# Sparse cross-attention and a trigonometric FFN on one core: thresholds in three Newton rounds, a reordered end, and two moved synchronisations

## The reference

```python
def sparsemax(x):
    zs = -jnp.sort(-x, axis=-1)
    cssv = jnp.cumsum(zs, axis=-1) - 1.0
    k = jnp.sum(zs > cssv / jnp.arange(1, L + 1), axis=-1)       # how many scores lie above tau
    tau = cssv[k - 1] / k
    return jnp.clip(x - tau, 0.0)

x = x + (sparsemax(q(layernorm(x)) @ k(ctx).T * 32**-0.5) @ v(ctx)) @ Wo + bo
n = layernorm(x)
x = x + sqrt((n @ cos(theta + theta_noise))**2 + (n @ sin(phi + phi_noise))**2)
```

## Time and profile before

| | before |
|---|---|
| median of 3 runs | 680.38 us (677.35 to 681.27) |
| profiled execution, its own time | 676.18 us |
| its span, first to last instruction | 674.4 us |
| mean granted TensorE clock | 0.915 |
| PE busy | 571.3 us (85%) |
| DVE busy | 573.3 us (85%) |
| ACT busy | 378.0 us (56%) |
| POOL busy | 189.0 us (28%) |
| HBM traffic | 38 GB/s over the span |

### The profile page before, as it was taken

The page is one execution under the profiler, slowest core; times in us unless marked ns, Lnnn a source line. Parts: engine busy times, 40 slices in busy tenths (PEclk is TensorE's granted clock), DMA queues, the critical chain, the costliest instruction groups (busy, mean ns, idle before and its releaser), DMA issues.

```text
span 674.4 us, 14485 instructions
## 1 busy us (share of the span) xinstructions
PE 571.3 (85%) x4648; PEld 336.7 (50%) x4648; DVE 573.3 (85%) x2900; ACT 378.0 (56%) x657; POOL 189.0 (28%) x239
## 2 busy tenths in 40 slices
PE   2686999999913999899999999991899999988675
PEld 1343665656502655565556555651556565645431
DVE  5699999978967999999999999995999999999400
ACT  3674568767511667566756676661466666554321
POOL 2711322332220250435133422342024431310301
PEclk9968987999965999999999999996899999996768
DMA  9863022302230103130323022302203020300000
GB/s 309 273 173 91 16 63 74 96 7 62 84 84 0 31 11 98 55 98 5 85 69 105 0 61 89 103 11 61 76 9 98 20 54 27 80 7 9 13 1 12
DMA packets 33506, 44.25 MB, mean 66 GB/s; under 512 B 8386, under 2 KB 26818, under 8 KB 33415
## 3 DMA queue, kind: packets, MB, share of 16 engines
q1 hardware_dynamic: 32332, 41.16, 21.4%
q10 hardware_dynamic: 1088, 2.10, 0.9%
HBM read 23.77 MB, written 1.64 MB: 38 GB/s over the span
## 4 chain that ended last, share of the span: by engine, by line
PE 49%; DVE 26%; issue 11%; ACT 7%; SPq 4%; DMA 2%; POOL 1%; DVEq 0%; POOLq 0%; ACTq 0%
PE ring L463 29%; DVE cand L952 7%; PE mix_bank L583 3%; PE ring L612 3%; DVE dif L966 3%; PE ring L514 3%; PE ring L558 3%; DVE f_sum L975 3%; SPq L255 3%; DVE over L969 3%; ACT S L692 3%; PE ring L531 2%; DVE n_over L977 2%; DVE dif L970 2%; PE ring L501 1%
## 5 line engine op out<-in xcount | busy, mean ns | idle before, releaser
L952 DVE MAX8 cand<-S 100x8 f32<-100x45 f32 (+1 forms) x2048 | 223.5, 195 | 2.1 <-issue 0.4
L463 PE MATMUL ring<-wv,ctx 128*121 128x512 f16 x576 | 154.5, 390 | 0.0
L463 PE MATMUL ring<-ctx,wk 128*128 128x361 f16 x768 | 125.7, 323 | 4.7 <-DVE ctx L1118 4.7
L817 ACT ACTIVATE pT<-ring 121x800 f32<-121x800 f32 x96 | 80.5, 839 | 72.3 <-PE ring L612 71.6
L692 ACT ACTIVATE S<-ring 100x722 f32<-100x722 f32 x128 | 95.5, 773 | 32.6 <-PE ring L558 32.6
L463 PEld LDWEIGHTS ring<-ctx,wk 128*128 128x128 f16 x768 | 75.1, 99 | 50.0 <-issue 7.1
L340 POOL TENSOR_TENSOR ctx<-ctx_f,ctx 128x484 f16<-128x484 f32 x42 | 51.5, 1225 | 149.8 <-ACT ctx L692 149.4
L463 PEld LDWEIGHTS ring<-wv,ctx 128*121 128x121 f16 x576 | 71.4, 136 | 34.0 <-issue 7.7
L348 POOL TENSOR_TENSOR ks<-k_f,ks 128x361 f16<-128x361 f32 x64 | 57.9, 905 | 79.6 <-ACT k_f L704 76.7
L558 PE MATMUL ring<-kst,qst 96*100 96x361 f16 x256 | 65.1, 348 | 11.5 <-DMA kst<-ks 8.9
L612 PEld LDWEIGHTS ring<-qst,kst 99*121 99x121 f16 x768 | 59.3, 147 | 29.7 <-issue 13.8
(11 more groups left out here) (124 smaller groups left out, 722.9 us busy)
## 6 DMA issues: line engine op xcount, KB each, us to landing
kst<-ks SPq DMA_DIRECT2D x384, 45.1 KB, 1.9
ctx_f<-in_ctx SPq DMA_DIRECT2D x45, 242.0 KB, 2.9
xq<-in_x SPq DMA_DIRECT2D x8, 200.0 KB
xr<-in_x SPq DMA_DIRECT2D x8, 200.0 KB
out_y<-att SPq DMA_DIRECT2D x8, 200.0 KB
S<-in_L_xattn_Wk ACTq DMA_DIRECT2D x1, 1024.0 KB, 6.9
wq<-in_L_xattn_Wq ACTq DMA_DIRECT2D x1, 1024.0 KB, 11.4
wcos<-in_L_ffn_theta SPq DMA_DIRECT2D x1, 1024.0 KB, 10.4
```

The lines of the kernel that those rows point to most:

```text
L463: last = nc.tensor.matmul(psum, lhs(c, i), w(c, j), start=(c == 0 and n == 0), stop=(c == DC - 1 and n == 2))
L817: nc.scalar.activation(pT[0:CK, u % 3, :, :], src, ACT.Relu).then_inc(two_read, 1)
L952: last = nc.vector.max(pieces[:, h, :, n], S[0:L, HH * (i % 2) + h, cuts[n]:cuts[n + 1]])
```

## The change

Five edits are made together.

1. `thresholds` makes three rounds over 3, 6 and 7 ranks instead of four over 2, 4, 6 and 7. The start is 0.9 of the old one plus 0.1 of the row's largest score. The second round's step is stretched by 1.12 and the result held at or under the largest score. Marks are written in fp32 beside the positive parts, so that one sum over both gives f and the count.
2. The test compares the count of the last round with the count at the final tau on DVE, row by row (`changed`), and the final step may be negative. PE then sums `changed` and the marks of rank 8: two matmuls instead of nine.
3. After an odd phase `sum_flags` stands in the next phase behind K's first projection instead of at the end of its own.
4. POOL waits for DVE's norm of x (`xn_ready`) before the last three of the six low contexts.
5. The end: `o_of` waits block by block, and three of its four blocks are put into the last `attend`; DVE adds the residual straight from PSUM, adds the squares, and makes the last sum; two FFN steps of phase 15 move back.

```diff
-RANKS = (2, 4, 6, 7)
-STRETCH = (1.15, 1.1, 1.0, 1.0)
+RANKS = (3, 6, 7)
+STRETCH = (1.0, 1.12)
+TOWARDS_MAX = 0.1
 # POOL
                         for kc in range(KC):
+                            if kc == KC // 2:
+                                pool.wait_ge(xn_ready, b + 2)
                             low_ctx(b + 1, kc)
                     if b > 0:
                         residual(b - 1)
+                    if 0 < b < B:
                         attended_x(b - 1)
-            y_of(B - 1)
 # PE
             def o_of(b):
-                pe.wait_ge(aT_ready, DC * (b + 1))
                 for c in range(DC):
+                    pe.wait_ge(aT_ready, DC * b + c + 1)
             def sum_flags(i):
-                nc.tensor.matmul(flag_ps[:, :, PIECES], ones[:, :], n_over[:, :], start=True, stop=True)
-                for r in range(8):
-                    last = nc.tensor.matmul(flag_ps[:, :, 0:PIECES], (one_b if r == 7 else minus_b)[:, :],
-                                            marks[:, :, r, :], start=(r == 0), stop=(r == 7))
+                nc.tensor.matmul(flag_ps[:, :, PIECES], ones[:, :], changed[:, :], start=True, stop=True)
+                nc.tensor.matmul(flag_ps[:, :, 0:PIECES], one_b[:, :], marks[:, :, 7, :], start=True,
+                                 stop=True).then_inc(flag_sum, 1)
 ...
-                    fill = chain(itertools.islice(queries, 3), x2, queries, ffn)
+                    idle = iter([None] * (0 if b + 1 < B else 2))
+                    fill = chain(itertools.islice(queries, 3), x2, queries, idle, ffn)
 ...
                     weave(heads, fill, 1)
-                    if 0 <= i < NH:
-                        sum_flags(i)
                 else:
                     if b < B:
                         run(k_of(b, 2, 0), 4)
+                    if i > 0:
+                        sum_flags(i - 1)
+                    if b < B:
                         run(k_of(b, 2, 1), 4)
 ...
+                    attended_o = o_of(b - 1) if b > 0 else iter(())
                     run(fill, 4)
+                    if b == B:
+                        run(attended_o, 1)
                     for n, _ in enumerate(units):
                         run(fill, 2 if n == 0 else 1)
+                        if b == B and n in (0, 10):
+                            run(attended_o, 1)
                     weave(heads, fill, 1)
-                    if b > 0:
-                        run(o_of(b - 1), 4)
+                    run(attended_o, 4)
                     if i < NH:
                         sum_flags(i)
 # DVE, thresholds
+                counted(nc.vector.tensor_reduce(top[:, :], cand[:, :, 0:PIECES], AX, ALU.max))
+                n = counted(nc.vector.tensor_reduce(f_sum, cand[:, :, 0:PIECES], AX, ALU.add))
+                n = counted(nc.vector.tensor_scalar(t, f_sum, -1.0, (1.0 - TOWARDS_MAX) / PIECES, ALU.add, ALU.mult))
+                n = counted(nc.vector.scalar_tensor_tensor(t, top[:, :], TOWARDS_MAX, t, ALU.mult, ALU.add))
                 for turn, ranks in enumerate(RANKS):
+                    n = counted(nc.vector.tensor_tensor(above, cand[:, :, 0:E], t3.broadcast_to([L, HH, E]), ALU.subtract))
+                    counted(nc.vector.tensor_scalar(member, above, 0.0, TINY, ALU.is_ge, ALU.max))
+                    n = counted(nc.vector.tensor_scalar(above, above, 0.0, None, ALU.max))
+                    n = counted(nc.vector.reduce_sum(sums[:, :, :], dif[:, :, :, 0:E], AX))
+                    n = counted(nc.vector.reciprocal(step_t[:, :], n_over))
                     ...
+                    if turn < len(RANKS) - 1 and STRETCH[turn] > 1.0:
+                        n = counted(nc.vector.tensor_tensor(t, t, top[:, :], ALU.min))
+                nc.vector.tensor_tensor(t, step_t[:, :], t, ALU.add).then_inc(tau_ready, 1)
+                n = counted(nc.vector.tensor_tensor(over[:, :, :], cand[:, :, :], t3.broadcast_to([L, HH, NCAND]), ALU.is_ge))
+                n = counted(nc.vector.reduce_sum(n_still[:, :], over[:, :, 0:PIECES * max(RANKS)], AX))
+                nc.vector.tensor_tensor(changed[:, :], n_still[:, :], n_over, ALU.not_equal).then_inc(flag_ready, 1)
 # DVE, the end
+            def last_x():
+                dve.wait_ge(one_full, one["o", B - 1] + 1)
+                dve.wait_ge(res_ready, B)
+                dve.wait_ge(y_ready, B - 1)
+                nc.vector.tensor_tensor(x1[:, :], ring1[0:L, one["o", B - 1] % 3, :], xr[:, :], ALU.add).then_inc(one_read, 1)
+            def last_y():
+                dve.wait_ge(one_read, seen1(("ffn", B - 1, 1)))
+                nc.vector.tensor_tensor(sq[:, 1, :], sq[:, 0, :], sq[:, 1, :], ALU.add).then_inc(sqsum_ready, 1)
+                dve.wait_ge(root_ready, B)
+                nc.vector.tensor_tensor(att[:, :], x1[:, :], sq[:, 0, :], ALU.add).then_inc(y_ready, 1)
```

More of the change, by code:

```diff
@@ L151, in build_kernel @@
         cand = sb("cand", [L, HH, NCAND])
-        dif, over = sb("dif", [L, HH, PIECES * max(RANKS)]), sb("over", [L, HH, NCAND], BF16)
-        fold = sb("fold", [L, HH, 2 + PIECES * max(RANKS) // 2], BF16)
+        dif = sb("dif", [L, 2, HH, PIECES * max(RANKS)])
+        over = dif[:, 1, :, :].bitcast(BF16)[:, :, 0:NCAND]
         tau = sb("tau", [L, 2, HH])
-        f_sum, step_t, n_over = (sb(n, [L, HH]) for n in ("f_sum", "step_t", "n_over"))
+        sums = sb("sums", [L, 2, HH])
+        f_sum, n_over = sums[:, 0, :], sums[:, 1, :]
+        step_t, top = sb("step_t", [L, HH]), sb("top", [L, HH])
         zero = sb("zero", [L, 1])
-        one_b, minus_b = sb("one_b", [L, 1], BF16), sb("minus_b", [L, 1], BF16)
+        n_still, changed = sb("n_still", [L, HH]), sb("changed", [L, HH])
+        one_b = sb("one_b", [L, 1], BF16)
         bit_c, code, lost = (sb(n, [1, HH]) for n in ("bit_c", "code", "lost"))
@@ L167, in build_kernel @@
         st2, mv2, sd2 = sb("st2", [L, 6]), sb("mv2", [L, 2]), sb("sd2", [L, 2])
-        relu_row = dif[:, :, :].rearrange("p g n -> p (g n)")[:, 0:N]
-        mask_row = over[:, :, :].rearrange("p g n -> p (g n)")[:, 0:N]
+        relu_row = dif[:, :, :, :].rearrange("p a g n -> p (a g n)")[:, 0:N]
+        mask_row = dif[:, 1, :, :].rearrange("p g n -> p (g n)").bitcast(BF16)[:, 0:N]
         marks = over[:, :, :].rearrange("p g (r n) -> p g r n", r=8)
@@ L963, in thresholds @@
+                after(n)
+                n = counted(nc.vector.scalar_tensor_tensor(t, top[:, :], TOWARDS_MAX, t, ALU.mult, ALU.add))
                 for turn, ranks in enumerate(RANKS):
                     E = PIECES * ranks
+                    above, member = dif[:, 0, :, 0:E], dif[:, 1, :, 0:E]
                     after(n)
-                    n = counted(nc.vector.tensor_tensor(dif[:, :, 0:E], cand[:, :, 0:E],
-                                                        t3.broadcast_to([L, HH, E]), ALU.subtract))
+                    n = counted(nc.vector.tensor_tensor(above, cand[:, :, 0:E], t3.broadcast_to([L, HH, E]), ALU.subtract))
@@ L968, in thresholds @@
                     after(n)
[L969 to L973, removed]
@@ L982, in thresholds @@
+                    n = counted(nc.vector.tensor_scalar(above, above, 0.0, None, ALU.max))
+                    after(n)
+                    n = counted(nc.vector.reduce_sum(sums[:, :, :], dif[:, :, :, 0:E], AX))
+                    after(n)
+                    n = counted(nc.vector.reciprocal(step_t[:, :], n_over))
+                    after(n)
+                    n = counted(nc.vector.scalar_tensor_tensor(step_t[:, :], f_sum, -1.0, step_t[:, :],
                                                                ALU.add, ALU.mult))
@@ L1085, in ln2_stats @@
             def ln2_stats(b):
-                dve.wait_ge(x1_ready, b + 1)
+                if b < B - 1:
+                    dve.wait_ge(x1_ready, b + 1)
+                else:
+                    dve.wait_ge(one_read, seen1(("o", b)))
                 stats(b, x1, st2, mv2, ln2_stat)
+            def last_x():
+                dve.wait_ge(one_full, one["o", B - 1] + 1)
+                dve.wait_ge(one_read, one["o", B - 1])
+                dve.wait_ge(res_ready, B)
[5 more added lines that the diff above has]
+                dve.wait_ge(root_ready, B)
+                dve.wait_ge(stored, 16 * (B - 1))
+                nc.vector.tensor_tensor(att[:, :], x1[:, :], sq[:, 0, :], ALU.add).then_inc(y_ready, 1)
             def ln2_apply(b):
@@ L1130, in _ @@
             nc.vector.memset(one_b[:, :], 1.0).then_inc(dve_const, 1)
-            nc.vector.memset(minus_b[:, :], -1.0).then_inc(dve_const, 1)
             for h in range(HH):
                 counted(nc.vector.memset(bit_c[:, h:h + 1], 2.0 ** h))
-            n = [counted(nc.vector.memset(again[:, :], 0.0)), counted(nc.vector.memset(zero[:, :], 0.0)),
-                 counted(nc.vector.memset(fold[:, :, 0:2], TINY))][-1]
+            n = [counted(nc.vector.memset(again[:, :], 0.0)), counted(nc.vector.memset(zero[:, :], 0.0))][-1]
             after(n)
```

(2 more changed lines are left out.)

22 lines of the change are left out of this document (6 added, 16 removed).

## The result

The changed kernel takes 1978.89 us (median of 4 runs, 1976.77 to 1979.38), the kernel before 679.2: a ratio of 2.91, 95% interval 2.90 to 2.92. It was forecast at 658.5, with 712 as the upper end.

What follows compares the result with a forecast made beforehand. DVE was taken to set the pace, with PE having 1.6 us of slack. Gains of 1.6 + 10.5 + 0.8 + 5.0 + 4.0 = 21.9 us took the profiled 676.18 to 654.3, a median of 658.5; range 631 to 712.

Steps and rivals of the forecast that it cites:

- the sum's last condition: Flag test: the summed gain of 21.9 us assumed that three heads are still refined, as before.
- the rivals: Other outcomes: more flagged heads 0.28, fewer 0.12, GpSimd's queue taking the gain 0.12, slow marks 0.04.
- The price of a head: Refinement of a flagged head: 16 us alone, 11 more as a second one, because PE stands behind `verified`.
- The thresholds: DVE's undisturbed threshold pass: 16.2 us for 16.57, so 0.4 us less for each half-batch.
- The pair: Quiet pair of half-batches, 69.3 us: 2.1 us less, bounds 0.8 and 2.4; five such pairs give 10.5.
- The 1.0 of the collisions: DVE instructions beside GpSimd's low contexts: the new wait wins 1.0 us for a pair, bounds 0 and 1.5.
- the 0.8 of the thresholds: DVE's saving in a pair from the new threshold passes, 0.4 us for each half-batch.
- DVE sets the pace: Quiet pair: DVE is the limit and PE has 1.6 us of slack in 69.3.
- GpSimd's queue: Rival, chance 0.12: low contexts delay the tau split and x, PE or DVE waits about 1 us a pair; 668.
- The end: After the last flag sum: 2.5 from the output projection, 1.3 and 1.2 from sums on DVE; together 5.0 us.
- the clock: PE's clock in `attend(15)` and behind: a shorter pause might keep 2.4 GHz; 4 us gained, bounds 0 and 8.
- the stage ahead of the pairs: Ahead of 178 us, where PE is the limit: three flag sums and one pass, 1.6 us gained.

Runs made afterwards that it cites:

- e9_stretch_third: The kernel before with only the third of its four rounds stretched by 1.12 instead of 1.0; 1129.17 us in a single run.
- e2_no_stretch: The changed kernel with the second round's step not stretched (1.0 for 1.12); 1431.2 us in a single run.
- e4_count_blind: The changed kernel with the count compared with itself, so only full pieces flag a head; 642.06 us, ratio 0.944 to the kernel before.
- e6_flag_sum_moved: The kernel before with only the flag sums of odd phases moved behind K's first projection; 671.36 us, ratio 0.988.
- e5_low_ctx_wait: The kernel before with only GpSimd's wait for the norm ahead of the last three low contexts; 679.39 us, ratio 1.000.
- e8_third_round_7: The old four rounds with the third over 7 ranks instead of 6, plus both moved waits and the new end; 651.5 us, ratio 0.959 to the kernel before.
- e10_no_ctx_wait: Old four rounds, third over 7 ranks, with moved flag sums and new end but without GpSimd's wait for the norm; 654.93 us, ratio 0.964 to the kernel before.
- e1_old_rounds: The changed kernel with the old four rounds, test and nine-matmul flag sum, keeping both moved waits and the new end; 664.91 us, ratio 0.977 to the kernel before.
- e7_new_end: The kernel before with only the new end: block-wise output projection, DVE residual and sums, two FFN steps back; 666.48 us, ratio 0.981.

## Why the prediction was wrong

**The step that failed** is the sum's last condition, "all of this leaves three refined heads in place". The mechanism that broke it stands among the rivals: a row that had all but arrived is put 12% of its step beyond tau, and a candidate in the gap flags the head. By the replay that is what happened in each of the 120 heads: 81% of all rows stood beyond tau before the last step, and 367 of them had a candidate in the gap. The runs showed 120 refined heads for the three of the sum, at 11.3 us each. I gave it 0.28 and, within it, 0.14 to anything above four heads, arguing that the start lies closer and that full pieces might be the cause of the three. Both are partly true (two of the three heads stay flagged in every run whose rounds converge) and neither bears on the matter. What I did not do is put numbers to the test as I had to DVE's instructions. The test asks not whether tau is good but whether no candidate lies between the tau of the last round and the final one, for all 100 rows of a head. So a head is flagged as soon as one row in a hundred is not finished one round early: even a 1% chance for a row, if the rows are independent, gives 63% of the heads. A stretch ahead of the test puts every row that still moves at that risk, on either side of tau: too far in the changed kernel, thrown back too far in `e9_stretch_third` (3 to 38 heads by it alone). Three rounds leave the risk without a stretch too, then of being short (`e2_no_stretch`: 66).

**The price of a head** was forecast at 11 to 16 us, 14 on average; it is 11.3 in the changed kernel, with 7.5 heads in a half-batch on average, and 12.9 in `e9_stretch_third`, with 2.4. That fits the prediction's dearer first head. The prediction held that two more heads would undo everything; the run had 117 more.

**The thresholds.** Forecast 16.2 us. In `e4_count_blind` a pass is 16.89 from 379.65 to 396.54, 0.73 of it a collision of L989 with GpSimd's low half of the queries, which the prediction's undisturbed pass does not have; without it 16.16. The timeline of that run:

```profile
379.65 0.29 DVE L970 TENSOR_REDUCE top<-cand 100x8 f32<-100x128 f32 x1
...
383.05 0.90 DVE L989 SCALAR_TENSOR_TENSOR step_t<-sums,step_t 100x8 f32<-100x8 f32 x1
...
386.23 1.75 DVE L985 TENSOR_REDUCE sums<-dif 100x16 f32<-100x1536 f32 x1
...
389.99 0.63 DVE L982 TENSOR_SCALAR dif<-dif 100x896 f32<-100x896 f32 x1
...
391.19 2.02 DVE L985 TENSOR_REDUCE sums<-dif 100x16 f32<-100x1792 f32 x1
...
396.54 3.63 DVE L962 MAX8 cand<-S 100x8 f32<-100x45 f32 x33
```

The joint sums take the 1.75 and 2.0 that the line through the earlier trace rows gave, and the mark with two operations and an fp32 output (L982) takes the 0.63 that the one-operation L969 takes in the earlier trace rows.

**The pair.** Forecast 2.1 us less, bounds 0.8 and 2.4. In `e4_count_blind` a quiet pair takes 66.8 for 69.28:

```profile
365.73 0.20 PE L548 MATMUL mix_bank<-changed,ones 100*1 100x8 f32 x2
...
432.54 0.20 PE L548 MATMUL mix_bank<-changed,ones 100*1 100x8 f32 x2
```

That is 2.46 less, just outside the bounds: all of PE's slack (1.6, as in `e6_flag_sum_moved`) and both shortened flag sums (0.8). The size was near, the parts were not. The 1.0 of the collisions brought nothing by itself (`e5_low_ctx_wait`) and counts only where DVE is in front, as in two pairs of `e8_third_round_7` against `e10_no_ctx_wait`; the 0.8 of the thresholds is seen in no pair. "DVE sets the pace" was the wrong reading of the earlier trace rows: the two pauses shown there, PE's behind DVE and DVE's behind ACT, were two ends of one loop.

**GpSimd's queue** as a rival is out: in `e5_low_ctx_wait` x and the low halves of K come as far behind the pair's first flag sum as without the wait, and nothing waits for them.

**The end.** Forecast 5.0 without the clock and 0 to 8 with it. From the last flag sum to the end it was 43.6 us; it is 37.2 in `e1_old_rounds`, where `attend(15)` still ran at 1.2 GHz, and 32.3 in `e7_new_end`, where most of it ran at 2.4: gains of 6.4 and 11.3. The one DVE sum out of PSUM, the price that no row of before had, is 0.69 us (forecast 0.7):

```profile
1958.12 0.69 DVE L1112 TENSOR_TENSOR x<-ring,xr 100x512 f32<-100x512 f32 x1 [17.94 <-PE ring L520]
```

By the 120 cycles of the Trainium skill, "VectorE: DVE Perf Modes", section "The TRN2 errata", the estimate was 0.66; the trace of the changed kernel has 0.03 more.

**The sum without the heads.** The profiled executions of `e4_count_blind` and of the kernel before span 642.8 and 674.4 us, 31.6 apart. The missing head is 9.8 to 11.9 of that. Its pair went from 96.5 to 84.3, and the range is open because a quiet pair gained 2.46 and the other pair with a head only 0.4. That leaves 19.7 to 21.8 for the forecast 21.9, but the terms did not all come so: the five pairs gave 8.2 to 10.3 for 10.5, the end 11.5 for 9.0, and the stage ahead of the pairs with the last two half-batches nothing for 2.4. That the total fits is in part luck.

## What to carry to other kernels

Where a fast path has a test and a slow path, the rate at which the test fires is a term of the sum like any other, and often the largest: count it from the data before pricing instructions, because a test over a whole group (here 100 rows) multiplies a small chance for each member. Do not over-relax the step ahead of a test for convergence, and look at what the test cannot see: one whose last step is held at or above 0 passes every row that was put too far. And when two engines each show one short pause in a period, follow the loop that joins them before calling one of them the bound: an edit pays if it cuts the loop, as the moved flag sum did, and not because it shortens the busier engine.

## What was not expected of the hardware

In `e1_old_rounds` PE paused 1.72 us ahead of the last flag sum, and its next small matmuls came at 1.2 GHz; in `e7_new_end` the pause was 0.76 us and they came at 2.4 GHz. In the earlier trace rows it was 3.51, and also 1.2 GHz afterwards. The lines of the two runs:

```profile
627.21 0.19 PE L544 MATMUL mix_bank<-n_over,ones 100*1 100x8 f32 x2 [1.72 <-DVE over L996]
...
629.92 0.83 PE L602 MATMUL ring<-ident,tt 100*3 100x100 f16 x8 [1.00 <-POOLq L398]
```
```profile
629.34 0.20 PE L542 MATMUL mix_bank<-n_over,ones 100*1 100x8 f32 x2 [0.76 <-DVE over L993]
...
632.19 0.52 PE L600 MATMUL ring<-ident,tt 100*3 100x100 f16 x8 [1.14 <-POOLq L398]
```

The flag sums and a block of the output projection between the pause and these matmuls ran at full clock in both, so a pause of 1.72 us with another of 1.00 soon behind it was followed by the lower clock. The second pause does not decide it. `e8_third_round_7` and `e10_no_ctx_wait` have the same 1.00; the first, with 1.68 ahead of the flag sum, fell to 1.2 GHz and came back within `attend(15)`, and the second, with 1.13, did not fall:

```profile
616.91 0.20 PE L544 MATMUL mix_bank<-n_over,ones 100*1 100x8 f32 x2 [1.68 <-DVE over L996]
...
619.62 0.82 PE L602 MATMUL ring<-ident,tt 100*3 100x100 f16 x8 [1.00 <-POOLq L398]
```
```profile
620.00 0.19 PE L542 MATMUL mix_bank<-n_over,ones 100*1 100x8 f32 x2 [1.13 <-DVE over L994]
...
622.71 0.52 PE L600 MATMUL ring<-ident,tt 100*3 100x100 f16 x8 [1.00 <-POOLq L398]
```

The difference between `e1_old_rounds` and `e7_new_end` is worth some 5 us of the end, and it moved between runs whose code at the end is the same.
